# Turning the first half's norms by DMA instead of on TensorE, with the second norm's transfers behind head 4's

## The chip, the cores and the metric

One core of a Trainium2 chip. The metric is the device time of one execution in microseconds; the kernel before took 1820.86 us (median of 3 runs, 1820.22 to 1822.54). The engines of the core work side by side, each through its own queue of instructions in order: TensorE (matmuls, with its weight loads shown apart), VectorE, ScalarE, GpSimd, and SyncE, which here only issues DMA transfers. They meet at semaphores.

## The reference

`x` and a context are 16 batches of 256 rows of 256 numbers. Four residual layers follow each other; the change lies in the first one:

```
x = x + L0_xattn(ctx, layernorm(x), ...)      # first half
x = x + L0_ffn(layernorm(x), ...)             # second half, from here on
x = x + L1_xattn(layernorm(x), ctx, ctx, ...)
x = x + L1_ffn(layernorm(x), ...)             # 8 experts, routed

def L0_xattn(x, latents, ...):
    xn = layernorm(x) * gamma_media + beta_media
    ln = layernorm(latents) * gamma_lat + beta_lat
    q  = ln @ Wq + bq
    k, v = split(concat([xn, ln]) @ Wkv + bkv)      # 512 rows of keys and values
    out = softmax(q k^T / sqrt(128)) v              # 8 heads of width 128
    return out @ Wo + bo
```

Here the "media" input is the context (norm 0, `k` = 0 in the code) and the latents are x, normalised twice (norms 1 and 2; the second has `k` = 1 where only two inputs are counted). Gamma and beta belong to columns of the normalised rows.

## The kernel before

**Precision.** Each matmul operand is held as two fp32r halves, a high one (ScalarE rounds) and a low one (VectorE subtracts the high from the full value). A product of two such operands is three matmuls (L741 to L743).

**The first half** (`latent_attention`) has a turn for each batch b of 16. Within it eight heads follow each other. In head h's step TensorE computes the scores of head h+1 (`sim`), then the step's products into a ring of four PSUM banks, in the order of `slot`: K of head h+2, Q in even steps, O of head h-1, V. From head 6 on, K, Q and V are already those of batch b+1. ScalarE takes exps and high halves, VectorE maxima, low halves and inverses of row sums, GpSimd the normalisation of the probabilities. The probabilities go from rows to columns by DMA: GpSimd writes a high f16 part (L411), VectorE the low one (L665), SyncE issues a transposing transfer for each (`cross`, L323), ScalarE casts both back to fp32r (`casts`, L512). `cross(b, h)` waits for the part to be made and for the cast that frees its buffer.

**The norms of batch b+1** are made in turn b: statistics on VectorE in steps 0 to 2, the norm's application on GpSimd (`norm_apply`, L400) in the same steps. In step 4, after the first product, TensorE transposes both norms (`transposes`, L752: eight 128x128 transposes into the banks `ps_c` and `ps_x`). ScalarE applies gamma and beta out of these banks into `aff` (L459, two activations for each norm, after the second and third product of step 4). In step 5 VectorE splits `aff` into `kvh` and `kvl` (`kv_halves`, L591 and L593): for norm 0 ahead of the step's products, for norm 1 after the first. TensorE waits for both (`kv_ready`) before the first product of step 6, K of head 0 of the next batch.

**Order and extras.** Nothing reorders these queues; they are written out. In turns 1 to 8 (the `spare` loop) one expert's weights of the second half are loaded, split by ScalarE (steps 0 to 2) and VectorE (L1891, steps 1 to 3) and stored. Turn 14 prepares the second half (`ahead`), and turn 15 has no next batch and runs work of the second half beside its own (`beside`). There the probabilities are transposed on TensorE. GpSimd fills the second half's weights in `early`, `ahead` and `beside`: rank-one updates, then an accumulating DMA (`weights_added`, L1258).

**The end of the first half.** TensorE projects the last batch out in four groups, with the second half's products at the marks `("W", 0)` and `("W", 1)`: the transposes of that half's norm C, and the products that need them.

The second half already turns its own norm A by DMA in the same manner: `ln_parts`, `ln_turned`, L1734, L1208, L1430.

## Time and profile before

| | |
|---|---|
| median of 3 runs | 1820.86 us |
| the profiled execution | 1820.83 us, span 1818.9 us |
| TensorE, matmuls | 1785.6 us busy, 98% |
| VectorE | 1467.5 us, 81% |
| ScalarE | 1329.6 us, 73% |
| GpSimd | 548.0 us, 30% |
| granted TensorE clock | full in every slice |

The span is cut into engines' busy times; TensorE's matmuls overlap, so its busy share is not its distance to its peak. The first half ends at about 984 us. In timelines a row gives the start, the duration, the engine and line, the operation and its output and input, and in brackets the idle time of the engine before it and what ended it. Two starts that follow each other give the pitch, which is shorter than the duration because instructions overlap.

### The profile page before, as it was taken

Reading aid. Unit: us, or ns where it says so; the run is one execution under the profiler, and the core shown is the slowest. Engines: PE = TensorE matmul, PEld = TensorE weight load, DVE = VectorE, ACT = ScalarE, POOL = GpSimd, SP = SyncE. Lnnn points to the kernel's source line nnn. Section 1 sums busy time; section 2 is a strip of 40 time slices with the busy share of each in tenths; the row PEclk is TensorE's granted clock in tenths of the full one; section 3 lists DMA queues with packets and bytes.
Section 4 is the critical chain, followed back from the end, with each engine's and each line's share of the span. In section 5 each row is a group of like instructions: output and inputs, shape, how many; then the busy total and the mean of one; then the engine's idle time right before and its main releaser. Section 6 shows DMA issues by size and latency. Waiting matters only on the chain.

```text
span 1818.9 us, 40134 instructions
## 1 busy us (share of the span) xinstructions
PE 1785.6 (98%) x12818; PEld 1658.1 (91%) x12818; DVE 1467.5 (81%) x3544; ACT 1329.6 (73%) x2554; POOL 548.0 (30%) x714
## 2 busy tenths in 40 slices
PE   7999999999999999999999999999999999999999
PEld 5888888888888888888888999999999999999998
DVE  7888888888888878888667888888888888888876
ACT  5778777877887777777777767777767777776653
POOL 3454434543345433454542111101111110111100
PEclk9999999999999999999999999999999999999999
DMA  5565555545555444444529534333443434344300
GB/s 151 109 134 124 124 135 133 148 103 145 133 133 99 87 93 86 97 96 91 117 68 311 147 66 95 72 88 72 83 94 66 95 69 90 72 83 89 72 7 13
DMA packets 370652, 185.92 MB, mean 102 GB/s; under 512 B 307744, under 2 KB 355744, under 8 KB 370592
## 3 DMA queue, kind: packets, MB, share of 16 engines
q1 hardware_dynamic: 361888, 150.55, 34.9%
q0 software_dynamic: 8704, 34.61, 10.5%
q8 instruction: 33, 0.54, 0.1%
q14 instruction: 27, 0.22, 0.0%
HBM read 97.29 MB, written 21.23 MB: 65 GB/s over the span
## 4 chain that ended last, share of the span: by engine, by line
PE 81%; DVE 8%; ACT 4%; issue 4%; DMA 2%; POOL 1%; SPq 0%; DVEq 0%; ACTq 0%; POOLq 0%
PE ring L741 9%; PE ring L743 9%; PE ring L742 9%; PE ring L2087 8%; PE ring L2089 8%; PE ring L2088 8%; PE sim L2089 3%; PE sim L2087 3%; PE sim L2088 3%; PE sim L741 3%; PE sim L742 2%; PE sim L743 2%; PE ps_x L741 2%; PE ps_x L742 2%; PE ps_x L743 2%
## 5 line engine op out<-in xcount | busy, mean ns | idle before, releaser
L411 POOL TENSOR_SCALAR a_parts<-a_pr,a_rinv 128x512 f16<-128x512 f32 x240 | 177.8, 752 | 468.3 <-DVE a_rinv L656 420.0
L2087 PE MATMUL ring<-b_xch,b_wel 128*128 128x256 f32 x1024 | 288.6, 282 | 0.5 <-DVE b_act_e L1701 0.5
L2089 PE MATMUL ring<-b_xcl,b_weh 128*128 128x256 f32 x1024 | 286.4, 280 | 0.0
L2088 PE MATMUL ring<-b_xch,b_weh 128*128 128x256 f32 x1024 | 286.2, 279 | 0.0
L2088 PEld LDWEIGHTS ring<-b_xch,b_weh 128*128 128x128 f32 x1024 | 193.4, 189 | 0.0
L2087 PEld LDWEIGHTS ring<-b_xch,b_wel 128*128 128x128 f32 x1024 | 192.2, 188 | 0.7 <-DVE b_act_e L1701 0.7
L2089 PEld LDWEIGHTS ring<-b_xcl,b_weh 128*128 128x128 f32 x1024 | 192.0, 188 | 0.0
L504 ACT ACTIVATE a_pr<-sim,a_nmax 128x512 f32<-128x512 f32 x256 | 173.7, 688 | 19.4 <-DVE a_nmax L645 18.8
L1407 ACT ACTIVATE b_heh<-b_act_e 128x512 fp32r<-128x512 f32 x128 | 80.9, 632 | 136.0 <-DVE b_act_e L1701 114.6
L665 DVE SCALAR_TENSOR_TENSOR a_parts<-a_pr,a_rinv,a_parts 128x512 f16<-128x512 f32 x240 | 178.8, 786 | 0.0
L645 DVE TENSOR_REDUCE a_nmax<-sim 128x1 f32<-128x512 f32 x256 | 165.0, 682 | 9.8 <-PE sim L743 9.8
L741 PE MATMUL ring<-a_pth,a_vh 128*128 128x256 f32 x512 | 146.4, 286 | 1.9 <-ACT a_ptl L512 0.5
L512 ACT ACTIVATE a_ptl<-a_turned 128x1024 fp32r<-128x1024 f16 x120 | 127.0, 1058 | 26.1 <-DMA a_turned<-a_parts 26.0
L492 ACT ACTIVATE a_vh<-ring 128x512 fp32r<-128x512 f32 x128 | 77.0, 601 | 90.9 <-PE ring L743 90.9
L742 PE MATMUL ring<-a_ptl,a_vh 128*128 128x256 f32 x512 | 143.0, 279 | 0.0
L743 PE MATMUL ring<-a_pth,a_vl 128*128 128x256 f32 x512 | 142.9, 279 | 0.0
L1227 POOL TENSOR_SCALAR b_rows<-b_mv 128x2 f32<-128x2 f32 x48 | 12.5, 260 | 430.7 <-DVE b_mv L1641 430.5
L632 DVE TENSOR_TENSOR a_vl<-ring,a_vh 128x512 fp32r<-128x512 f32 x128 | 88.2, 689 | 59.5 <-ACT a_vh L492 59.4
L623 DVE SCALAR_TENSOR_TENSOR a_ktl<-ring,a_bkv_s,a_kth 128x512 fp32r<-128x512 f32 x128 | 96.0, 750 | 48.0 <-ACT a_kth L484 46.0
L1701 DVE TENSOR_TENSOR b_act_e<-b_act_e,ring 128x512 f32<-128x512 f32 x128 | 87.6, 684 | 51.7 <-PE ring L2089 39.1
L512 ACT ACTIVATE a_pth<-a_turned 128x1024 fp32r<-128x1024 f16 x120 | 127.3, 1061 | 2.3 <-DMA a_turned<-a_parts 2.2
L1403 ACT ACTIVATE b_act_e<-ring 128x512 f32<-128x512 f32 x128 | 76.1, 595 | 60.6 <-PE ring L2089 60.3
(369 smaller groups left out, 6473.6 us busy)
## 6 DMA issues: line engine op xcount, KB each, us to landing
b_w2l_raw<-in_W2T POOLq DMA_DIRECT2D x16, 1088.0 KB, 8.8
b_even_b<-rows_between SPq DMA_DIRECT2D x16, 1024.0 KB, 5.5
b_w1l_raw<-in_W1T POOLq DMA_DIRECT2D x16, 1024.0 KB, 8.4
b_w1l_raw<-in_We SPq DMA_DIRECT2D x8, 768.0 KB, 4.6
expert_halves<-b_w1h SPq DMA_DIRECT2D x8, 768.0 KB, 3.5
expert_halves<-b_w1l SPq DMA_DIRECT2D x8, 768.0 KB, 4.9
b_weh<-expert_halves SPq DMA_DIRECT2D x8, 768.0 KB, 8.7
b_wel<-expert_halves SPq DMA_DIRECT2D x8, 768.0 KB, 10.2
```

The source lines that it names most:

```text
L411: nc.gpsimd.tensor_scalar(parts[:, 0, t, :], pr[:, h % 2, t, :], rinv[:, h % 2, t:t + 1], 1.0, ALU.mult, ALU.mult).then_inc(prob_ready, 1)
L504: nc.scalar.activation(pr[:, h % 2, t, :], sim[t][:], ACT.Exp, bias=nmax[:, h % 2, t:t + 1], accum_out=rsum[:, h % 2, t:t + 1]).then_inc(e ...
L512: nc.scalar.activation(dst[:].rearrange("p k (t q) -> p t k q", t=ST), turned[:, part], ACT.Copy, scale=1.0 / PART_SCALE).then_inc(cast, 1)
L623: nc.vector.scalar_tensor_tensor(ktl[:, h % 2], bank[:], bkv_s[:, 0, h:h + 1], f32(kth[:, h % 2]), ALU.add, ALU.subtract).then_inc(ring_lo, 1)
L645: nc.vector.tensor_reduce(nmax[:, h % 2, t:t + 1], sim[t][:], AX.X, ALU.max, negate=True)\
L665: nc.vector.scalar_tensor_tensor(parts[:, 1, t, :], pr[:, h % 2, t, :], rinv[:, h % 2, t:t + 1], parts[:, 0, t, :], ALU.mult, ALU.subtract ...
L741: nc.tensor.matmul(out, lh, rh, start=(begins and n == 0), stop=False)
L742: nc.tensor.matmul(out, lh, rl, start=False, stop=False)
L743: last = nc.tensor.matmul(out, ll, rh, start=False, stop=(ends and n == len(parts) - 1))
L2087: nc.tensor.matmul(out, ll, rh, start=(n == 0), stop=False)
L2088: nc.tensor.matmul(out, lh, rh, start=False, stop=False)
L2089: last = nc.tensor.matmul(out, lh, rl, start=False, stop=(n == len(parts) - 1))
```

## The change

- `ln_crossing` reserves 8704 bytes in the region `low` for f16 parts of both norms (`a_ln_parts`), their turned form (`a_ln_turned`), and gamma divided by 2^11 (`gms`, `gls`).
- For batches 1 to 15 TensorE no longer transposes the norms; only batch 0's stay there.
- GpSimd writes the high part of norm 0 in step 0 and that of norm 1 in step 3 (`ln_high`). VectorE writes the low parts after step 2's last product and after step 4's second (`ln_low`).
- SyncE issues two transfers for each norm, those of norm 0 behind head 2's probabilities and those of norm 1 behind head 4's (`ln_cross`).
- ScalarE applies gamma and beta to the turned high part after the last product of steps 3 and 5 (`affine_high`).
- VectorE adds the turned low part times gamma, then splits (`joined_halves`), for norm 0 ahead of step 5's products, for norm 1 after the second product.
- The wait for `x1_ready` moves to the projection in step 5. On GpSimd eight memsets move to the begin of the last turn, and `weights_added(0, "1")` from step 7 to step 6 of turn 14. At the end of the first half the mark `("W", 0)` comes right after the first group of projections.

```diff
+        def ln_cross(b, k):
+            take(kv_ready, b * 2 - 1 + k)
+            for part in range(2):
+                take(ln_part, (b - 1) * 4 + 2 * k + part + 1)
+                sp.dma_start_transpose(ln_turned[:, k, part].rearrange("p t c q -> p (t c) q"),
+                                       ln_parts[:, k, part].rearrange("p t d -> p (t d)")).then_inc(lnT_ready, 16)
...
                 if nxt and h + 1 < H:
                     cross(b, h + 1)
+                if nxt and h in (1, 3):
+                    ln_cross(b + 1, h // 2)
...
+        def ln_high(b, k):
+            take(ln_ready, b * 3 + 2 * k + 1)
+            if k == 1:
+                take(ln_part, (b - 1) * 4 + 2)
+            nc.gpsimd.tensor_scalar(ln_parts[:, k, 0], (c_ln, x_ln2)[k][:], LN_SCALE, 1.0, ALU.mult, ALU.mult)\
+                .then_inc(ln_part, 1)
...
                 if nxt and h < 3:
                     rstd_of(b + 1, h)
                     norm_apply(b + 1, h)
+                    if h == 0:
+                        ln_high(b + 1, 0)
+                if nxt and h == 3:
+                    ln_high(b + 1, 1)
...
+        def affine_high(b, k):
+            g, bb = ((gms, bm), (gls, bl))[k]
+            act.wait_ge(lnT_ready, (b - 1) * 64 + 2 + 32 * k + 32)
+            for c in range(DC):
+                last = nc.scalar.activation(aff[:, k, c, :].rearrange("p (t q) -> p t q", t=ST), ln_turned[:, k, 0, :, c, :],
+                                            ACT.Identity, bias=bb[:, c:c + 1], scale=g[:, c:c + 1])
             last.then_inc(aff_ready, 1)
...
-                    if j == 1 and h == H - 4 and nxt:
-                        affine(b + 1, 0)
-                    if j == 2 and h == H - 4 and nxt:
-                        affine(b + 1, 1)
+                    if j == n - 1 and h == 3 and nxt:
+                        affine_high(b + 1, 0)
+                    if j == n - 1 and h == H - 3 and nxt:
+                        affine_high(b + 1, 1)
...
+        def ln_low(b, k):
+            dve.wait_ge(ln_part, (b - 1) * 4 + 2 * k + 1)
+            nc.vector.scalar_tensor_tensor(ln_parts[:, k, 1], (c_ln, x_ln2)[k][:], LN_SCALE, ln_parts[:, k, 0],
+                                           ALU.mult, ALU.subtract).then_inc(ln_part, 1)
+
+        def joined_halves(b, k):
+            done = (b - 1) * 4 + 2 + 2 * k
+            dve.wait_ge(aff_ready, b * 2 + k + 1)
+            for c in range(DC):
+                last = nc.vector.scalar_tensor_tensor(
+                    aff[:, k, c, :].rearrange("p (t q) -> p t q", t=ST), ln_turned[:, k, 1, :, c, :], (gms, gls)[k][:, c:c + 1],
+                    aff[:, k, c, :].rearrange("p (t q) -> p t q", t=ST), ALU.mult, ALU.add)
+            last.then_inc(kv_hi, 1)
+            dve.wait_ge(kv_hi, done + 1)
+            nc.vector.tensor_copy(kvh[:, :, k * S:(k + 1) * S], aff[:, k]).then_inc(kv_hi, 1)
+            dve.wait_ge(kv_hi, done + 2)
             nc.vector.tensor_tensor(kvl[:, :, k * S:(k + 1) * S], aff[:, k], f32(kvh[:, :, k * S:(k + 1) * S]),
                                     ALU.subtract).then_inc(kv_ready, 1)
...
-                    kv_halves(b + 1, 0)
+                    joined_halves(b + 1, 0)
...
-                    if j == 0 and h == H - 3 and nxt:
-                        kv_halves(b + 1, 1)
+                    if j == 1 and h == H - 3 and nxt:
+                        joined_halves(b + 1, 1)
...
+                    if j == n - 1 and h == 2 and nxt:
+                        ln_low(b + 1, 0)
+                    if j == 1 and h == 4 and nxt:
+                        ln_low(b + 1, 1)
...
-                    if j == 0 and h == H - 4 and nxt:
-                        if prev:
-                            pe.wait_ge(x1_ready, b)
-                        transposes(b + 1)
...
+                other.beside(H, ("W", 0))
                 project_out(b, order, i + 1, 1, range(H - 1))
                 project_out(b, order, i + 1, 0, range(H - 1, H))
-                other.beside(H, ("W", 0))
                 project_out(b, order, i + 1, 1, range(H - 1, H))
```

## Rows read from the trace of the kernel before

**Rows 1.** The page: busy times, and the chain that ended last by engine.

```profile
PE 1785.6 (98%) x12818; PEld 1658.1 (91%) x12818; DVE 1467.5 (81%) x3544; ACT 1329.6 (73%) x2554; POOL 548.0 (30%) x714
PE 81%; DVE 8%; ACT 4%; issue 4%; DMA 2%; POOL 1%; SPq 0%; DVEq 0%; ACTq 0%; POOLq 0%
```

**Rows 2.** Windows: stretch, length, busy (count) PE PEld DVE ACT POOL, clock, DMA.

```profile
734.60:791.60 57.00, 56.97 (x346) 49.98 (x346) 46.35 (x99) 44.00 (x85) 25.12 (x30) 1.00 0.44 92
448.80:506.50 57.70, 57.38 (x346) 50.08 (x345) 48.31 (x101) 45.74 (x88) 25.27 (x30) 1.00 0.55 132
```

**Rows 3.** Timeline of TensorE in a plain turn, at heads 4, 5 and 6.

```profile
748.14 0.60 PE L752 MATMUL ps_c<-ident,a_c_ln 128*128 128x128 f32 x4
...
748.93 0.36 PE L741 MATMUL ring<-a_kvh,a_wqh 128*128 128x256 f32 x1
749.13 0.28 PE L742 MATMUL ring<-a_kvl,a_wqh 128*128 128x256 f32 x1
...
755.75 0.39 PE L743 MATMUL ring<-a_kvh,a_wkl 128*128 128x512 f32 x1
756.16 0.38 PE L741 MATMUL ring<-a_pth,a_vh 128*128 128x256 f32 x1
...
761.88 0.39 PE L741 MATMUL ring<-a_kvh,a_wkh 128*128 128x512 f32 x1
```

**Rows 4.** VectorE there, heads 3 to 6, and the low parts' line from 740 to 750.

```profile
744.40 0.75 DVE L623 SCALAR_TENSOR_TENSOR a_ktl<-ring,a_bkv_s,a_kth 128x512 fp32r<-128x512 f32 x1 [0.59 <-ACT a_kth L484]
...
750.09 0.75 DVE L623 SCALAR_TENSOR_TENSOR a_ktl<-ring,a_bkv_s,a_kth 128x512 fp32r<-128x512 f32 x1 [0.21 <-ACT a_kth L484]
...
751.50 0.88 DVE L627 SCALAR_TENSOR_TENSOR a_qtl<-ring,a_bq_s,a_qth 128x256 fp32r<-128x256 f32 x2 [0.39 <-ACT a_qth L488]
752.90 0.69 DVE L632 TENSOR_TENSOR a_vl<-ring,a_vh 128x512 fp32r<-128x512 f32 x1 [0.53 <-ACT a_vh L492]
754.17 0.48 DVE L639 SCALAR_TENSOR_TENSOR a_otl<-ring,a_bkv_s,a_oth 128x256 fp32r<-128x256 f32 x1 [0.58 <-ACT a_oth L497]
754.57 1.28 DVE L645 TENSOR_REDUCE a_nmax<-sim 128x1 f32<-128x512 f32 x2
...
757.09 0.42 DVE L591 CAST a_kvh<-a_aff 128x512 fp32r<-128x512 f32 x1
757.55 0.69 DVE L593 TENSOR_TENSOR a_kvl<-a_aff,a_kvh 128x512 fp32r<-128x512 f32 x1
...
759.57 0.69 DVE L593 TENSOR_TENSOR a_kvl<-a_aff,a_kvh 128x512 fp32r<-128x512 f32 x1
...
L665 DVE SCALAR_TENSOR_TENSOR a_parts<-a_pr,a_rinv,a_parts x4: 740/752/1194, 742.4 to 749.1; 128x512 f16<-128x512 f32 x4
```

**Rows 5.** ScalarE in the same turn: head 3's low cast, norm 1's affine.

```profile
747.07 1.06 ACT L512 ACTIVATE a_ptl<-a_turned 128x1024 fp32r<-128x1024 f16 x1
...
752.74 1.04 ACT L459 ACTIVATE a_aff<-ps_x,a_bl,a_gl 128x256 f32<-128x256 f32 x2
```

**Rows 6.** The second half's instructions of this kind (min/median/max in ns).

```profile
L1734 DVE SCALAR_TENSOR_TENSOR b_ln_parts<-b_ln,b_ln_parts x14: 681/684/686, 1023.9 to 1715.3; 128x512 f16<-128x512 f32 x14
L1430 ACT ACTIVATE b_xth<-b_ln_turned x14: 632/632/635, 1028.1 to 1720.6; 128x512 fp32r<-128x512 f16 x14
```

**Rows 7.** The probabilities' transfers: SyncE's issue (ns), and time to landing.

```profile
L323 SPq DMA_TRANSPOSE a_turned<-a_parts x240: 1231/1232/2204, 31.8 to 888.5; - x120
...
DMA to landing us min/median/max: 3.1/3.1/4.9
```

**Rows 8.** An expert turn: ScalarE and VectorE at head 4, TensorE at head 6.

```profile
289.24 1.07 ACT L512 ACTIVATE a_ptl<-a_turned 128x1024 fp32r<-128x1024 f16 x1 [1.03 <-DMA a_turned<-a_parts]
...
292.25 0.75 DVE L623 SCALAR_TENSOR_TENSOR a_ktl<-ring,a_bkv_s,a_kth 128x512 fp32r<-128x512 f32 x1 [0.54 <-ACT a_kth L484]
...
303.41 0.39 PE L741 MATMUL ring<-a_kvh,a_wkh 128*128 128x512 f32 x1
```

**Rows 9.** TensorE at the end of the first half, waiting for norm C.

```profile
983.30 0.39 PE L2178 MATMUL sim<-b_xch,b_wr 128*128 128x256 f32 x1 [1.12 <-DVE b_xcl L1730]
```

More of the change, by code:

```diff
@@ L78, in crossing, with ln_crossing @@
         return Region(low.nc, (low.top + 127) // 128 * 128 + 2 * 8 * KB + 64, 8 * KB)
+    def ln_crossing(self):
+        low = self.of["low"]
+        return Region(low.nc, (low.top + 127) // 128 * 128 + 2 * 8 * KB + 64 + 8704, 8704)
 @dataclass
@@ L397, in norm_apply @@
             if k != 1:
-                take(lnT_ready, b * 2 - 1 + k // 2)
+                take(lnT_ready, (b - 1) * 64 + 2)
             for t in range(ST):
@@ L460, in affine @@
                                             bias=bb[:, c:c + 1], scale=g[:, c:c + 1])
+            last.then_inc(aff_ready, 1)
+        def affine_high(b, k):
[4 more added lines that the diff above has]
+                                            ACT.Identity, bias=bb[:, c:c + 1], scale=g[:, c:c + 1])
             last.then_inc(aff_ready, 1)
@@ L822, in project_out @@
                 last.then_inc(wo_full, 1)
-        pe.wait_ge(consts, 1)
+        pe.wait_ge(pool_step, 3)
         transposes(0)
@@ L884, in fill_count @@
         return last.at(at + last.names[at:].index(name)) + 1
-    names = ("consts", "kv_ready", "x1_ready", "x1_out", "ring_full", "ring_lo", "sim_full", "exp_done", "wo_full", "took",
+    names = ("kv_ready", "x1_ready", "x1_out", "ring_full", "ring_lo", "sim_full", "exp_done", "wo_full", "took",
              "part_hi", "part_lo", "turned")
-    sems = dict(zip(names, (consts, kv_ready, x1_ready, x1_out, ring_full, ring_lo, sim_full, exp_done, wo_full, took,
+    sems = dict(zip(names, (kv_ready, x1_ready, x1_out, ring_full, ring_lo, sim_full, exp_done, wo_full, took,
                             prob_ready, part_lo, turned_lo)))
@@ L1270, in early @@
                 for e in range(E):
-                    nc.gpsimd.memset(index[:, e:e + 1], float(e))
-                for c in range(HC):
-                    last = nc.gpsimd.memset(f32(w2_raw[:, c * W2ROW + D:(c + 1) * W2ROW]), 0.0)
+                    last = nc.gpsimd.memset(index[:, e:e + 1], float(e))
                 last.then_inc(consts, 1)
@@ L1287, in ahead @@
                 update(0, "1", 3)
+                weights_added(0, "1")
             if h == 7:
-                weights_added(0, "1")
                 rows_rstd(1)
@@ L1293, in beside @@
             if (h, done) == (0, "begin"):
+                pool.wait_ge(first.sems["kv_ready"], 2 * B)
+                for c in range(HC):
+                    nc.gpsimd.memset(f32(w2_raw[:, c * W2ROW + D:(c + 1) * W2ROW]), 0.0)
                 update(0, "2", 0)
```

19 lines of the change are left out of this document (14 added, 5 removed).

## The prediction

> **What bounds the kernel now.** I read the page first: TensorE is busy 98% of the span and carries 81% of the chain that ended last, with VectorE next at 8% [rows 1]. Then the busy times of whole turns of the first half [rows 2]. A turn is one batch of heads: 57.0 us for batches whose turn has nothing extra, 57.7 us for the eight turns that also split expert weights. TensorE has 56.97 us of work in the 57.0, so there the turn is as long as TensorE's queue. VectorE has 46.35 us and ScalarE 44.00: slack on average, which says nothing of a single head. So I read the timelines of TensorE, VectorE and ScalarE over heads 2 to 6 of one plain turn (batch near 734 to 792 us) and of one expert turn (near 276 to 334 us). What the reader is to see there: where VectorE and ScalarE have no idle gap left (a bracket on a row is the idle time before it), because the change takes work from TensorE and gives it to exactly these two.
>
> **What leaves TensorE.** The eight 128x128 transposes stand between the K and the Q product of head 4: from 748.14 to 748.93 us, 0.79 us [rows 3]. The product behind them starts 0.20 us before its successor instead of the usual 0.12: 0.87 us in all. A second piece: at head 5 the O product starts 0.41 us after the last K product (755.75 to 756.16), where 0.23 is the pitch of such a product [rows 3]; it had waited for ScalarE's cast of the low probabilities, which was late because the two affine pairs (1.04 us, 0.9 to the next start, the second at 752.74 [rows 5]) had pushed it. They move to heads 3 and 5, so these 0.18 us, and 0.10 of a slow first matmul behind them, are free as well. TensorE's own queue gets 1.15 us shorter per turn, 15 turns: 17.3 us. That is the most the edit can bring in the first half.
>
> **What VectorE gets.** Two low halves of the norms (`ln_low`) and, in `joined_halves`, four scalar_tensor_tensors of 128x256, which add the turned low half to the affine before the two instructions that were there already. `ln_low` is the instruction that the second half has: 0.684 us [rows 6], 0.60 to the next start. Back-to-back instructions of VectorE start about 0.09 us before the one ahead ends (0.48 long, 0.40 to the next start: 754.17 to 754.57 [rows 4]); the sums below go by such pitches. No row shows a 128x256 one that reads f16 from SBUF. The nearest is the Q pair, 0.88 us for two [rows 4]; the next instruction waits for its result, which costs 0.04 more (as from 757.09 + 0.42 to 757.55 [rows 4]): 0.92 us a pair. Bounds: not less than the 0.42 us of the cast over the same 512 elements, not more than 1.3, since one 512-element instruction with two inputs reached 1.19 us beside GpSimd [rows 4].
>
> **Head 2 and 3.** `ln_low(0)` sits behind head 2's last product, in front of the maxima of head 4 (741.20). The gap of 0.59 us before K's low half (744.40) takes it up for K [rows 4], but the low probability parts of head 3, between the two, end 0.60 us later, and their transfer lands 3.1 us behind its issue [rows 7]. SyncE also has the norm's second transfer in front: ready at 741.2 + 0.68 = 741.9, 1.23 us of issue each for it and for head 3's high part, so free again at 744.5, just when the low parts are (744.4): no cost, but no slack. ScalarE gets the first affine pair ahead of head 3's two casts: 0.7 us from the f16 source (the second half's 512-element one takes 0.632 [rows 6]). Bounds: 0.63 to the 0.9 of today. Its low cast (747.07, without idle time in front [rows 5]) starts 0.7 us later by either of the two, which overlap. Everything behind it on ScalarE shifts: exps of head 5, then K's high half, whose taker on VectorE goes from 750.09 to 750.79. Bounds of the shift: 0 (if the cast had slack) to 1.3 (both in series).
>
> **Head 4.** From K's low half to the maxima of head 6 VectorE now needs 0.66 (K), 0.29 (inverses), 0.79 (Q), 0.61 (V), 0.40 (O) and the new 0.60: 3.35 us. The three waits there today (0.39 on ScalarE's Q half, 0.53 and 0.58 [rows 4]) came from the affine pairs and from TensorE's transposes and go. Maxima of head 6: 754.14 instead of 754.57 [rows 4].
>
> **Head 5, where it is decided.** TensorE may not start the next batch's K product (761.88 today [rows 3]) before both halves of the keys' input are split. Today this is done at 759.57 + 0.69 = 760.26 [rows 4], 1.6 us early. Now from 754.14: maxima 1.20, parts 1.32, first joined halves 0.92 + 1.07, K's low 0.66, inverses 0.29, O's low 0.40 (the second joined halves stand behind it now), second joined halves 0.92 + 0.46 + 0.69: 7.93 us, so 762.07. With 0.15 for the wake-up and 0.10 for the slower first product TensorE goes on as if from 762.32. Without the wait it would be there at 760.73. So 1.6 us of new idling eat the 1.15 saved: +0.44 us a turn. VectorE's later gaps at heads 6 and 7 let it catch up, so the next turn starts in the same posture.
>
> **Expert turns.** VectorE there has no gap from head 1 to head 4. The low cast of head 3 already waits 1.03 us for its transfer [rows 8] and comes 0.60 later; K's low half 292.25 becomes 292.85; + 3.35 + 7.93 = 304.13; + 0.25 = 304.38 against 303.41 [rows 8]: +0.97 us. Its two stalls before the scores of heads 4 and 5 only move inside this.
>
> **The rest.** GpSimd gets two 128x512 conversions while it idles most of the span (30% busy [rows 1]): nothing; without that cover the probabilities of one head would be late by such a conversion. Issues of four more transfers a turn: nothing, as reckoned above; uncovered, each would be 1.23 us on the path of a cast. Two 128x2 activations at the start: under 0.5 us, beside loads. At the seam `weights_added` moves one step up on GpSimd; its issue and the next head's normalisation only swap places ahead of the row statistics for which VectorE waits, so the end of the three is the same: nothing. The eight small memsets go where GpSimd soon waits for VectorE: nothing. The last change moves the transposes of the final norm in front of 21 projection products (21 x 0.117 = 2.5 us); the 1.12 us that TensorE waits after them today and its restart [rows 9] go: -1.3 us, once.
>
> **Sum.** 8 expert turns x 0.97 = 7.8 (batch 0's turn, loaded with weight splits, counted as plain), 7 others x 0.44 = 3.1, seam -1.3: +9.6 us. The profiled execution took 1820.83 us around its span of 1818.9; the median of the runs is 1820.86, the same. Forecast 1830.4 us.
>
> **A rule weighed.** The longest of four low-part instructions took 1.194 us against a median of 0.752 [rows 4], and such pairs fall where GpSimd works. The Trainium skill, page "GPSIMD Engine Reference", Specifications, says that GpSimd shares its SBUF interfaces with VectorE and that they collide when a VectorE instruction has two SBUF inputs. The row agrees. By the rule the joined pairs, which run beside GpSimd's normalisation of heads 5 and 6, would be slow as well, and the sum would be the third rival's 1842; by the quiet row it stays at 1830.4.
>
> **Rivals.** (1) *The shift at head 3 is absorbed* (transfer and affine fit into slack that the timeline doesn't show): 0.7 and 0.6 less. Plain turns -0.26, expert turns +0.37: 7 x -0.26 + 8 x 0.37 - 1.3 = -0.2 us, 1820.6. For it: the cast follows its neighbour without a gap, so a small change of order could hide it; against it: the same in expert turns is plainly a wait for the transfer. (2) *Faster: the split is ready before TensorE asks.* It decides at the next batch's K product: if the chain of 7.93 us and what precedes it is 1.6 us shorter in plain turns, TensorE keeps the 1.15. The pairs at 0.42 give 1.0 of it, the absorbed shift 0.7: together enough. Then 15 x 1.15 + 1.3 = 18.6 us less; the expert turns, whose chain is 0.5 us longer, keep about 0.5 of it less (4 us): 1806. With only half of that margin, 1814. For it: VectorE's average load; against: no row with so cheap a pair. (3) *Slower still: the added two-input instructions collide with GpSimd*, pairs at 1.3: 0.76 more per turn, 11.4 us, 1842. For: the 1.194 row; against: only a part of them lies beside GpSimd. (4) *Transfers in SyncE's queue bound head 3*: a norm transfer lands or issues late (the second half's take longer under load) and the head's low part behind it by 1 us: +15, 1845.
>
> **Chances.** Forecast 0.52 (own range 1824.5 to 1838), rival 1 0.19, rival 2 with its half 0.19, rivals 3 and 4 together 0.10. No change is within 0.2%, 3.6 us, about what a measurement of this kernel can tell. Faster 0.19, same 0.20, slower 0.61. The range 1811 to 1841 leaves out the full rival 2 (0.09) and the tail of rivals 3 and 4 (0.06).
>
> **What would show it.** Right: the first-half 128x128 transposes fall from 128 to 8; TensorE idles about 1.6 us (less its restart) before the next batch's K product, released by VectorE's last `a_kvl`; the O product of head 5 no longer lags; head 3's low cast starts later; a turn lasts 57.4 plain and 58.6 with experts; the second half keeps its length. Wrong: turns of 56 us, or the wait at another product (scores of head 5 on `a_ktl`, O on the cast), or joined pairs away from 0.92 us.

## The result: 1841.9 us, 1.2% slower

The changed kernel took 1841.88 us (median of 4, 1840.66 to 1845.51), the kernel before 1821.51 beside it: ratio 1.0118, 95% interval [1.0106, 1.0130]. The forecast was 1830.4 us, the range 1811 to 1841. The sign and the place of the new wait were right; the loss was twice the forecast one (+20.4 us against +9.6).

The page after: busy times, and the chain that ended last, as [rows 1].

```profile
PE 1776.8 (97%) x12698; PEld 1645.7 (90%) x12698; DVE 1522.0 (83%) x3634; ACT 1331.0 (72%) x2556; POOL 574.7 (31%) x744
PE 63%; DVE 17%; issue 7%; ACT 5%; DMA 4%; SPq 2%; POOL 1%; DVEq 0%; ACTq 0%; POOLq 0%
```

120 transposes are gone from TensorE, and VectorE's share of the chain has doubled, from 8 to 17%. Where the time went is told by turns, from one write of `x_out` on VectorE to the next (differences to before, where the expert turns are 57.5 to 57.7 and the plain ones 56.9 to 57.1):

| stretch | after minus before, us |
|---|---|
| up to the first write | +3.6 |
| the turn after it (the first with an expert) | +2.0 |
| the 7 other expert turns | +8.2 (1.17 each) |
| 5 plain turns | +8.7 (1.74 each) |
| turn 14 and the last turn | -2.3 |
| all up to the last write | +20.1 |

The span grew by 19.9 (1818.9 to 1838.8), so in this execution the second half kept its length (the section on e7 comes back to that). Windows after of one plain and one expert turn, columns as in [rows 2]:

```profile
752.80:811.60 58.80, 56.55 (x337) 49.20 (x336) 50.20 (x105) 44.28 (x85) 27.21 (x32) 1.00 0.48 98
282.80:341.50 58.70, 56.60 (x337) 49.11 (x336) 51.81 (x108) 45.53 (x88) 26.65 (x32) 1.00 0.59 138
```

VectorE has 3.5 to 3.9 us more in a turn, ScalarE as much as before; VectorE's slack on average is still 7 to 9 us. TensorE's waits from 60 to 900 us (us in total, times, longest), after:

```profile
PE ring L807 <- DVE a_kvl L655: 16.2, 13, 1.7
PE sim L807 <- DVE a_qtl L689: 8.0, 16, 1.9
PE sim L807 <- DVE a_ktl L685: 7.9, 9, 0.9
PE ring L807 <- ACT a_ptl L554: 2.6, 3, 1.5
```

The first row did not exist before: it is the forecast wait for the keys' input. In the same stretch of before the second was 0.8 us, once, and the third 2.4 us in 8. In the plain turn TensorE shows two waits, at the scores of head 6 and at K of the next batch (against 761.88 in [rows 3]; by the write of `x_out` at its head 1 this turn lies 18.86 us later than the one shown of before). At 767.32 Q follows K without the transposes, and at 775.10 O follows K at its usual pitch:

```profile
767.09 0.39 PE L809 MATMUL ring<-a_kvh,a_wkl 128*128 128x512 f32 x1
767.32 0.28 PE L807 MATMUL ring<-a_kvh,a_wqh 128*128 128x256 f32 x1
...
772.23 0.49 PE L807 MATMUL sim<-a_kth,a_qth 128*128 128x512 f32 x1 [0.54 <-DVE a_qtl L689]
...
774.87 0.39 PE L809 MATMUL ring<-a_kvh,a_wkl 128*128 128x512 f32 x1
775.10 0.28 PE L807 MATMUL ring<-a_pth,a_vh 128*128 128x256 f32 x1
...
782.49 0.50 PE L807 MATMUL ring<-a_kvh,a_wkh 128*128 128x512 f32 x1 [1.64 <-DVE a_kvl L655]
```

Both kernels run the same 336 other matmuls in a turn, in the same order. Laid beside each other from the write of `x_out`, the changed one gains and loses at five products (changed minus before, us, with the slower first matmuls behind a wait):

| TensorE's product | the plain turn | an expert turn (from 282.8) |
|---|---|---|
| scores of head 5 | +0.33 | +0.60 |
| Q in step 4, the transposes gone | -0.87 | -0.88 |
| scores of head 6 | +0.80 | +0.55 |
| O in step 5 | -0.28 | -0.29 |
| K of the next batch | +1.92 | +1.21 |
| sum | +1.90 | +1.19 |

VectorE in the plain turn, to be laid beside [rows 4]:

```profile
760.05 0.82 DVE L640 SCALAR_TENSOR_TENSOR a_ln_parts<-a_c_ln,a_ln_parts 128x512 f16<-128x512 f32 x1
...
762.00 1.64 DVE L727 SCALAR_TENSOR_TENSOR a_parts<-a_pr,a_rinv,a_parts 128x512 f16<-128x512 f32 x2
...
770.26 0.75 DVE L685 SCALAR_TENSOR_TENSOR a_ktl<-ring,a_bkv_s,a_kth 128x512 fp32r<-128x512 f32 x1 [1.24 <-ACT a_kth L526]
...
772.01 0.87 DVE L640 SCALAR_TENSOR_TENSOR a_ln_parts<-a_x_ln,a_ln_parts 128x512 f16<-128x512 f32 x1
...
773.79 1.27 DVE L707 TENSOR_REDUCE a_nmax<-sim 128x1 f32<-128x512 f32 x2
...
776.31 0.87 DVE L648 SCALAR_TENSOR_TENSOR a_aff<-a_ln_turned,a_gms,a_aff 128x256 f32<-128x256 f16 x2
777.21 0.43 DVE L653 CAST a_kvh<-a_aff 128x512 fp32r<-128x512 f32 x1
...
779.63 1.23 DVE L648 SCALAR_TENSOR_TENSOR a_aff<-a_ln_turned,a_gls,a_aff 128x256 f32<-128x256 f16 x2
780.90 0.81 DVE L653 CAST a_kvh<-a_aff 128x512 fp32r<-128x512 f32 x1
781.74 0.69 DVE L655 TENSOR_TENSOR a_kvl<-a_aff,a_kvh 128x512 fp32r<-128x512 f32 x1
```

Read the two joined pairs against each other: 0.87 us for the first, 1.23 for the second, and its cast 0.81 instead of 0.43. GpSimd and ScalarE beside them (the affine and low cast as in [rows 5]):

```profile
771.65 1.79 POOL L438 TENSOR_SCALAR a_parts<-a_pr,a_rinv 128x512 f16<-128x512 f32 x2 [1.48 <-DVE a_rinv L718]
779.66 1.76 POOL L438 TENSOR_SCALAR a_parts<-a_pr,a_rinv 128x512 f16<-128x512 f32 x2 [6.22 <-DVE a_rinv L718]
```

```profile
764.93 1.08 ACT L499 ACTIVATE a_aff<-a_ln_turned,a_bm,a_gms 128x256 f32<-128x256 f16 x2
...
767.25 1.06 ACT L554 ACTIVATE a_ptl<-a_turned 128x1024 fp32r<-128x1024 f16 x1 [0.29 <-DMA a_turned<-a_parts]
```

GpSimd's normalisations of heads 5 and 6 start with the low half of norm 1 and with the second pair; where they stand alone such a pair of GpSimd's takes 1.36 us, here 1.79 and 1.76. Both sides pay. In expert turns the second pair and its cast are quick, and GpSimd's normalisation of head 6 starts only behind them:

```profile
310.24 0.87 DVE L648 SCALAR_TENSOR_TENSOR a_aff<-a_ln_turned,a_gls,a_aff 128x256 f32<-128x256 f16 x2
311.15 0.43 DVE L653 CAST a_kvh<-a_aff 128x512 fp32r<-128x512 f32 x1
```

```profile
312.58 1.36 POOL L438 TENSOR_SCALAR a_parts<-a_pr,a_rinv 128x512 f16<-128x512 f32 x2 [8.54 <-DMA a_turned<-a_parts]
```

The norms' own transfers (issue in ns, time to landing), as [rows 7]:

```profile
L340 SPq DMA_TRANSPOSE a_ln_turned<-a_ln_parts x60: 1188/1189/2262, 48.2 to 891.7; - x60
...
DMA to landing us min/median/max: 2.4/2.4/4.2
```

### The profile page after: what moved, and what is told of

Same layout as the page of the kernel before. It is cut to its first block, busy times and chain, and to the rows that moved or that the text cites. A ratio compares the mean times of both kernels' runs of the same rounds, so it can differ in the third digit from the quotient of the medians.

```text
span 1838.8 us, 40340 instructions
## 1 busy us (share of the span) xinstructions
PE 1776.8 (97%) x12698; PEld 1645.7 (90%) x12698; DVE 1522.0 (83%) x3634; ACT 1331.0 (72%) x2556; POOL 574.7 (31%) x744
## 3 DMA queue, kind: packets, MB, share of 16 engines
q0 software_dynamic: 8704, 34.61, 10.5%
## 4 chain that ended last, share of the span: by engine, by line
PE 63%; DVE 17%; issue 7%; ACT 5%; DMA 4%; SPq 2%; POOL 1%; DVEq 0%; ACTq 0%; POOLq 0%
PE ring L2151 8%; PE ring L2153 8%; PE ring L2152 8%; PE ring L807 6%; PE ring L809 6%; PE ring L808 6%; DVE a_parts L727 3%; PE sim L2153 3%; PE sim L2151 3%; PE sim L2152 3%; DVE a_nmax L707 2%; DMA a_turned<-a_parts 2%; DVE a_aff L648 1%; PE ps_x L2151 1%; PE ps_x L2153 1%
## 5 line engine op out<-in xcount | busy, mean ns | idle before, releaser
L727 DVE SCALAR_TENSOR_TENSOR a_parts<-a_pr,a_rinv,a_parts 128x512 f16<-128x512 f32 x240 | 186.6, 817 | 3.2 <-DMA a_turned<-a_parts 1.9
L685 DVE SCALAR_TENSOR_TENSOR a_ktl<-ring,a_bkv_s,a_kth 128x512 fp32r<-128x512 f32 x128 | 95.8, 749 | 58.9 <-ACT a_kth L526 58.8
L807 PE MATMUL sim<-a_kth,a_qth 128*128 128x512 f32 x256 | 105.5, 412 | 20.1 <-DVE a_ktl L685 10.3
```

Of the source, the lines that this page charges most:

```text
L685: nc.vector.scalar_tensor_tensor(ktl[:, h % 2], bank[:], bkv_s[:, 0, h:h + 1], f32(kth[:, h % 2]), ALU.add, ALU.subtract).then_inc(ring_lo, 1)
L727: nc.vector.scalar_tensor_tensor(parts[:, 1, t, :], pr[:, h % 2, t, :], rinv[:, h % 2, t:t + 1], parts[:, 0, t, :], ALU.mult, ALU.subtract ...
L807: nc.tensor.matmul(out, lh, rh, start=(begins and n == 0), stop=False)
```

## The experiments

Differences are to the kernel before, measured beside each run (1819.4 to 1821.0 us); the changed kernel itself stands at +20.4. "Expert" and "plain" are the mean lengths of the 7 and 5 such turns of the table above in the profiled run (before 57.6 and 57.0, changed 58.8 and 58.8). e4, e7 and e12 are edits of the kernel before, the others of the changed one.

| run | edit | us | minus before | ratio, 95% interval | expert / plain |
|---|---|---|---|---|---|
| e4 | before, fewer transposes | 1812.5 | -7.1 | 0.9960 [0.9946, 0.9974] | 57.4 / 56.3 |
| e1 | no low halves | 1828.9 | +9.2 | 1.0049 [1.0032, 1.0066] | 57.7 / 57.9 |
| e2 | no joining | 1830.7 | +11.0 | 1.0063 [1.0047, 1.0080] | 58.2 / 57.6 |
| e3 | GpSimd waits, head 6 | 1836.2 | +16.5 | 1.0089 [1.0073, 1.0106] | 58.6 / 57.8 |
| e5 | low half 0 in step 1 | 1839.3 | +19.4 | 1.0102 [1.0086, 1.0119] | 58.5 / 58.6 |
| e9 | e5, bias in step 7 | 1841.9 | +20.8 | 1.0110 [1.0093, 1.0127] | 58.6 / 58.8 |
| e10 | e9 and e3 | 1836.4 | +15.4 | 1.0086 [1.0070, 1.0103] | 58.5 / 57.8 |
| e13 | e9, affine in a gap | 1837.7 | +18.2 | 1.0096 [1.0079, 1.0113] | 58.5 / 58.0 |
| e14 | e13, low half 1 in a gap | 1833.1 | +13.7 | 1.0063 [1.0047, 1.0080] | 58.3 / 57.6 |
| e15 | e14 and e3 | 1826.1 | +6.6 | 1.0033 [1.0022, 1.0045] | 58.3 / 56.8 |
| e17 | e15, low half 1 on GpSimd | 1827.1 | +6.8 | 1.0038 [1.0024, 1.0052] | 58.1 / 56.8 |
| e18 | e17, low half 0 too | 1826.7 | +6.4 | 1.0031 [1.0020, 1.0041] | 57.8 / 57.2 |
| e16 | e15, splits in step 6 | 1846.3 | +26.8 | 1.0142 [1.0125, 1.0159] | 60.6 / 56.9 |
| e8 | gamma, beta in rows | 1851.1 | +31.2 | 1.0161 [1.0141, 1.0181] | 59.7 / 58.4 |
| e11 | e8 spread | 1969.4 | +148.4 | 1.0808 [1.0790, 1.0826] | 68.8 / 64.4 |
| e6 | e5, affine, joining early | 1915.4 | +95.6 | 1.0516 [1.0497, 1.0534] | 63.8 / 63.5 |
| e7 | before, mark moved | 1820.3 | +0.4 | 1.0004 [0.9994, 1.0014] | 57.6 / 56.9 |
| e12 | before, bias in step 7 | 1820.8 | -0.2 | 0.9999 [0.9989, 1.0009] | 57.7 / 57.0 |

### What TensorE's saving is worth (e4)

```diff
-                        last = nc.tensor.transpose(ps[...], ln[:, t, c * P:(c + 1) * P], ident[:])
+                        if isinstance(b, int) and b == 0 or c == DC - 1 and t == ST - 1:
+                            last = nc.tensor.transpose(ps[...], ln[:, t, c * P:(c + 1) * P], ident[:])
```

> The kernel before with 2 of the 8 transposes of each batch from 1 on, one of each norm: six blocks of each batch's input stay those of batch 0, which leaves that part of the computation out. It measures what TensorE's saved time is worth where nothing is put in its place. Theory A (TensorE's queue sets the turn): six transposes of about 0.1 us each are 0.59 us a turn, 15 turns: 8.9 us less than 1821.5: 1812.6. Rival E (TensorE's saved time is lost anyway, because VectorE and ScalarE set the turn): 1821.

Six of eight transposes of each later batch are gone, and with them most of the turned norms: that part of the computation is left out. -7.1 us is 0.5 a turn, but it isn't spread evenly. Plain turns gain 0.75 us, so there the gain side of the change is real. Expert turns gain only 0.22: TensorE now waits 0.40 us in each for ScalarE's low cast, ahead of the O product of step 5. There a part of the saving is lost even with nothing put in its place.

### Taking one added cost away at a time (e1, e2, e3)

```diff
# e1: low halves over 4 elements only (but for the first batch)
+            n = D if isinstance(b, int) and b == 1 else 2
+            ... (c_ln, x_ln2)[k][:, :, 0:n], LN_SCALE, ln_parts[:, k, 0, :, 0:n], ...
# e2: joining over 2 elements only
+                    aff[:, k, c, 0:2], ln_turned[:, k, 1, 0, c, 0:2], (gms, gls)[k][:, c:c + 1], ...
# e3: GpSimd, ahead of the normalisation of head 6
+                if nxt and h == H - 3:
+                    take(kv_ready, b * 2 + 4)
```

> The changed kernel with VectorE's two low halves of the norms (ln_low) cut from 512 to 4 elements for all batches but the first turned one; transfers, joins and everything else stay. The rows joined are then partly old ones: that part of the computation is left out. Theory A (the loss comes from VectorE's chain: low half of norm 0 ahead of head 3's low probabilities, then the low half of norm 1 in head 4, each 0.75 to 0.79 us to the next start): 2 x 0.7 us less for each of 15 turns, 21 us less than the changed kernel's 1841.9: 1820 us, turns of 57.3 us. Rival B (the four more transfers in SyncE's queue set the end of head 3, the low half of norm 0 costs nothing): only norm 1's counts, 0.75 x 15 = 11 us less: 1831. Rival C (TensorE's stalls have another cause): 1842.

> The changed kernel with the four scalar_tensor_tensors per batch that add the turned low part (in joined_halves) cut from 256 to 2 elements: the low part of the norms is left out of the result. Theory A: the first pair costs 0.90 and the second, beside GpSimd, 1.27 us, and the cast behind it 0.38 more than it need: up to 2.2 us a turn come off the way to the next batch's K product, where TensorE idles 1.8 to 1.9 us in a plain turn and 1.2 in an expert turn; what is left is the stalls at the scores of heads 5 and 6 and TensorE's own queue of 55.9 us. 1841.9 less 7 x 1.8 and 8 x 1.2, 22 us: 1820 us. Rival B (the stall at that product is only moved, the scores' stalls grow): 1830 or more.

> The changed kernel, with one wait more: GpSimd starts the normalisation of head 6's probabilities only when VectorE has split the second norm (kv_ready), so that the two don't run side by side. The computation is whole. Theory A (collision of GpSimd with VectorE's two-input instructions costs 0.36 us in the second joined pair and 0.38 in the cast behind it): 0.74 x 15 = 11 us less than 1841.9: 1831 us, turns of 58.0 us, joined pair back at 0.87 us. Rival C (these instructions are slow by themselves at that place): 1842 and the same durations. Rival D (the later normalisation delays head 6's probabilities by 1.5 us and gives it all back): 1842 or more with the pair at 0.87.

Against the changed kernel's +20.4 the low halves are worth 11 us, the joining 9, the collision in step 5 alone 4: each about a third to a half of what theory A gave it. In every one of the three TensorE still waits for the last low half. No single term carries the loss; each lies on the same path. e1 and e2 leave a part of the computation out; in e3 nothing is, only GpSimd's one normalisation is later. Its plain turns fall by 0.9 us, of which the pair and the cast, back at 0.87 and 0.43, give 0.35 and 0.38; its expert turns, which had no such collision, fall by 0.1.

### A chain over two engines (e5, e9, e13, e14, e15)

```diff
# e5: VectorE's low half of norm 0
-                    if j == n - 1 and h == 2 and nxt:
+                    if j == n - 1 and h == 1 and nxt:
                         ln_low(b + 1, 0)
```

> The changed kernel, but norm 0's low half is made behind the last product of step 1 instead of step 2, so that its two transfers leave SyncE's queue before those of head 3's probabilities. Theory A (in plain turns half of the unforeseen loss comes from head 3: the low half in front of the maxima and the norm's second transfer in front of head 3's push its low cast by 1.3 us, and VectorE then idles 1.24 us at head 4 for K's high half): plain turns fall by 1.0 to 1.3 us, expert turns, where VectorE has no gap at head 1 either, by 0.3 to 0.5; about 1829. Rival B (only VectorE's load over heads 4 and 5 counts, the shift at head 3 is taken up anyway): less than 0.3 per turn, 1837 to 1841.

Only 0.15 to 0.25 a turn in the profiled run, and 1.0 us in the medians, which their spread doesn't separate. VectorE's wait of 1.24 us at head 4 was indeed gone, but the time was spent one instruction earlier. VectorE and GpSimd in e5:

```profile
765.16 2.62 DVE L727 SCALAR_TENSOR_TENSOR a_parts<-a_pr,a_rinv,a_parts 128x512 f16<-128x512 f32 x2
768.14 0.75 DVE L685 SCALAR_TENSOR_TENSOR a_ktl<-ring,a_bkv_s,a_kth 128x512 fp32r<-128x512 f32 x1 [0.36 <-ACT a_kth L526]
```

```profile
764.92 0.62 POOL L428 TENSOR_SCALAR a_ln_parts<-a_x_ln 128x512 f16<-128x512 f32 x1
765.62 1.61 POOL L448 TENSOR_TENSOR a_x_res<-a_x_res,a_bo_b 128x512 f32<-128x512 f32 x1
```

I took the 2.62 us (1.41 where GpSimd rests) for the cause and moved the bias addition away:

```diff
# e9
-                if h == 3:
+                if h == (7 if nxt else 3):
                     bias_residual(b, prev)
```

> The kernel with norm 0's low half in step 1 (1839.3) plus one move on GpSimd: the addition of the output bias to the residual (128x512, two inputs, 1.6 us) from step 3 to step 7. Theory A (VectorE's added instructions and its old two-input ones are slow because GpSimd works beside them; in that kernel the low parts of head 4 took 2.62 us for two beside this addition, and K's product of the next batch waits for what stands behind them): 0.8 to 1.2 us less per plain turn, 0.3 to 1.0 per expert turn; 1826 to 1830. Rival B (the pair is long because it waits for something else, the addition only lies beside it): 1838 to 1840.

The pair is quick again, and nothing is won: theory A fell. VectorE in e9, then ScalarE:

```profile
765.73 1.49 DVE L727 SCALAR_TENSOR_TENSOR a_parts<-a_pr,a_rinv,a_parts 128x512 f16<-128x512 f32 x2
768.71 0.75 DVE L685 SCALAR_TENSOR_TENSOR a_ktl<-ring,a_bkv_s,a_kth 128x512 fp32r<-128x512 f32 x1 [1.49 <-ACT a_kth L526]
```

```profile
763.29 0.60 ACT L534 ACTIVATE a_vh<-ring 128x512 fp32r<-128x512 f32 x1 [0.86 <-PE ring L809]
763.79 1.08 ACT L499 ACTIVATE a_aff<-a_ln_turned,a_bm,a_gms 128x256 f32<-128x256 f16 x2
764.77 1.04 ACT L554 ACTIVATE a_pth<-a_turned 128x1024 fp32r<-128x1024 f16 x1
765.72 1.04 ACT L554 ACTIVATE a_ptl<-a_turned 128x1024 fp32r<-128x1024 f16 x1
...
768.00 0.68 ACT L526 ACTIVATE a_kth<-ring,a_bkv_s 128x512 fp32r<-128x512 f32 x1
```

Here the path is in view. ScalarE waits 0.86 us for TensorE's V product of head 3; from there it has no gap through V's high half, the affine of norm 0 (0.98), two casts, the exps of head 5 and K's high half at 768.00. VectorE takes over at 768.71 and has no gap until the last low half. What is put between costs its full length; what is moved inside costs nothing. The 0.98 stands just behind the gap that could have hidden it:

```diff
# e13: ScalarE's affine of norm 0 ahead of V in step 3
-                    if j == n - 1 and h == 3 and nxt:
+                    if j == 1 and h == 3 and nxt:
                         affine_high(b + 1, 0)
# e14: VectorE's low half of norm 1 ahead of step 4's products
-                    if j == 1 and h == 4 and nxt:
-                        ln_low(b + 1, 1)
+                if h == 4 and nxt:
+                    ln_low(b + 1, 1)
```

e10 is e9 with e3's wait, e15 is e14 with it.

> As the run before (bias addition in step 7), and GpSimd's normalisation of head 6 waits until the joined halves are done, so that it no longer lies beside the second joined pair and its cast. Theory A (the same collisions, 1.0 us more per plain turn, little in expert turns, as the run with this wait alone showed): 7 us less than the run before, about 1820. Rival B (once the low parts of head 4 are quick, head 5 is no longer decided by VectorE's chain): within 2 us of the run before.

> The kernel with norm 0's low half in step 1 and the bias addition in step 7 (1841.9, turns of 58.55 with experts and 58.75 without) and one more move: ScalarE's affine of norm 0 before V's high half of head 3, where it idled 0.86 us for TensorE, instead of after it. Theory A (one serial chain over ScalarE and VectorE from V of head 3 to the next batch's K product decides; the affine stands in it with 0.98 us): plain turns 0.8 to 0.9 us less, expert turns 0.4 to 0.8; 1830. Rival B (the two engines are simply short of time in heads 3 to 5, order doesn't matter): 1840 to 1842.

> As the run before, and VectorE's low half of norm 1 ahead of step 4's products, where VectorE waits for ScalarE's K, instead of behind the second. Theory A: of 0.79 us the 0.5 that is still idle there is won, 0.5 per turn; 1824. Rival B: no change against the run before, since K's low half is pushed by as much.

> As the run before, and GpSimd's normalisation of head 6 waits for the joined halves (no collision in head 5; that wait alone took 5 us off in two earlier pairs of runs). Theory A: plain turns 56.4 to 56.9, expert turns 57.6 to 57.9; 1816 to 1820, at or just under the kernel before. Rival B: head 7 is late by the delayed probabilities once head 5 is no longer so, 1822 or more.

e10 gives 5.4 us over e9: the collision counts about as in e3 (3.9), not more. In e9, e13, e14 and e15 plain turns fell step by step, 58.8, 58.0, 57.6, 56.8, each within about 0.1 us of what theory A gave (0.8 to 0.9, 0.5, then the collision), and ended under the 57.0 of before. Expert turns did not follow: 58.6, 58.5, 58.3, 58.3. So the medians missed theory A each time: 1837.7 for 1830, 1833.1 for 1824, 1826.1 for 1816 to 1820. TensorE and VectorE in the plain turn of e15: the low half in the gap takes 0.68 instead of 0.87, and the pair and cast of norm 1 their undisturbed 0.87 and 0.43.

```profile
769.29 0.50 PE L809 MATMUL ring<-a_kvh,a_wkh 128*128 128x512 f32 x1 [0.56 <-DVE a_kvl L657]
```

```profile
757.45 0.68 DVE L642 SCALAR_TENSOR_TENSOR a_ln_parts<-a_x_ln,a_ln_parts 128x512 f16<-128x512 f32 x1
...
767.17 0.87 DVE L650 SCALAR_TENSOR_TENSOR a_aff<-a_ln_turned,a_gls,a_aff 128x256 f32<-128x256 f16 x2
768.08 0.43 DVE L655 CAST a_kvh<-a_aff 128x512 fp32r<-128x512 f32 x1
```

### Why expert turns don't follow (e16, e17, e18)

```diff
# e16: VectorE's second and third split in step 6, the stores in SyncE's step 7
-            if h in (1, 2, 3):
+            for n in {1: (0,), 6: (1, 2)}.get(h, ()):
# e17: the scale goes into the reciprocal deviation, GpSimd makes norm 1's low half in step 3
+            nc.gpsimd.tensor_tensor(ln_parts[:, k, 1], (c_ln, x_ln2)[k][:], ln_parts[:, k, 0],
+                                    ALU.subtract).then_inc(ln_part, 1)
# e18: and norm 0's in step 1
```

> As the run before, and in expert turns the second and third split of expert weights on VectorE in step 6 instead of steps 2 and 3 (their stores to DRAM in step 7 instead of 4). Theory A (expert turns lack the gaps of heads 2 and 3): expert turns become like plain ones, 0.6 to 1.0 less each, 1810 to 1813. Rival B (heads 6 and 7 have no room for 1.2 us either): no change.

e16 tells nothing of its question: the later stores stand in SyncE's way. Its issue of the next load comes at 273.7, 4.9 us behind the last store's, with the probabilities' transfers behind it, and TensorE waits up to 1.7 us, before scores, early in the turn that follows.

> The kernel with all moves (1826.1; turns of 58.35 with experts, 56.8 without), and the low half of norm 1 made by GpSimd behind the high half in step 3 instead of by VectorE in step 4 (the scale of 2^11 goes into the reciprocal deviation). Theory A (VectorE's serial work up to the last low half of the keys' input decides in both kinds of turn): expert turns 0.5 to 0.7 less, plain turns 0.4 to 0.6 until TensorE's own queue of 56.1 to 56.4 bounds; 1817 to 1820. Rival B (what VectorE is spared, the two-input instruction on GpSimd takes back by collision with the low parts of head 4): 1824 or more.

> As the run before, and norm 0's low half by GpSimd as well, behind its norm work in step 1. Theory A (expert turns also lose at the scores of heads 3 to 5 because VectorE has no gap in heads 1 to 4): expert turns another 0.3 to 0.6 less, plain ones unchanged; 1813 to 1817, faster than the kernel before. Rival B (GpSimd has 1.3 to 1.8 us of room in step 1, and the probabilities of head 3 come late): 1820 or more.

With both low halves off VectorE expert turns come to 57.8 us, near the 57.6 of before; with norm 1's alone off to 58.1. e1, which leaves the low halves out, has 57.7. So the two low halves, in heads where VectorE has no gap, are what held them. But GpSimd's two-input instruction takes part of it back: in e17 the low parts of head 4 lie beside it and last 2.40 us instead of 1.70 in e15, and plain turns gain nothing (in e18 they lose 0.4). VectorE in e15, then VectorE and GpSimd in e17:

```profile
755.83 1.70 DVE L729 SCALAR_TENSOR_TENSOR a_parts<-a_pr,a_rinv,a_parts 128x512 f16<-128x512 f32 x2
```

```profile
754.86 2.40 DVE L737 SCALAR_TENSOR_TENSOR a_parts<-a_pr,a_rinv,a_parts 128x512 f16<-128x512 f32 x2
```

```profile
755.23 1.49 POOL L435 TENSOR_TENSOR a_ln_parts<-a_x_ln,a_ln_parts 128x512 f16<-128x512 f32 x1
```

The profiled run of e18 is 7.1 us longer than that of before. 3.5 of them lie up to the second write of `x_out`, 1.2 in the expert turns (0.8 of that in one disturbed turn), 0.7 in the plain ones, -0.8 in turn 14 and the last, and 2.4 behind the last write of `x_out`, where the next section finds them again. In e15 it is 4.5 up to the last write and 3.1 behind it. Why the first turns, loaded with weight splits, cost more was not tried.

### Three ways that went wrong (e6, e8, e11)

```diff
# e6: e5, affine of norm 0 at the end of step 2, its joining at the end of step 3
# e8: GpSimd, on c_ln and x_ln2, g and b as rows of all 128 partitions
+                nc.gpsimd.tensor_tensor(dst[:], dst[:], g_row, ALU.mult)
+                nc.gpsimd.tensor_tensor(dst[:], dst[:], b_row, ALU.add)
# after the turn ScalarE casts the high half into kvh, VectorE the low one into kvl
# e11: these four in steps 1 to 3, all halves and transfers in steps 3 and 4
```

> As the run before (low half in step 1), and the affine of norm 0 behind the last product of step 2 and its two added two-input instructions behind the last product of step 3; only the split stays in step 5. Theory A (head 5 is decided by the chain on VectorE from the maxima to the last low half; 0.87 us less stand in it, but they are done at head 3 or 4, where VectorE has next to no gap left): 0.2 to 0.6 per plain turn better than the run before, nothing in expert turns; about 1827. Rival B (steps 3 and 4 have a gap that takes it whole): 0.87 x 15 = 13 us better than the run before, 1816.

> All norms of batches 1 to 15 by DMA, but gamma and beta are applied to the rows on GpSimd before the split into halves, so that after the turn ScalarE only casts the high half into the keys' input and VectorE the low half (behind step 5's second product); no affine and no joining. Low half of norm 0 in step 1. Theory A (the chain on VectorE in heads 4 and 5 is what costs; TensorE's saving of 1.15 us a turn comes through once it is gone): turns of 56.0 to 56.4 plain, 57.0 expert, 1804 with a range of 1801 to 1810. Rival B (turning by DMA costs by its transfers and by GpSimd's added work beside VectorE): 1815 or more.

> Gamma and beta applied to the rows on GpSimd, as in the run that took 1851.1 us, but GpSimd's four additions and multiplications (1.3 us each) are spread over steps 1 to 3, the high halves written in steps 3 and 4, the low halves at the ends of steps 3 and 4, the transfers in steps 3 and 4, the bias addition in step 7. After the turn only two casts on ScalarE and two on VectorE, in step 5. Theory A (that run was slow because GpSimd's norm work in steps 0 and 2 pushed the probabilities of heads 2 and 4): turns of 56.3 to 57.2; 1806 to 1815. Rival B (each two-input instruction on GpSimd costs VectorE more than it spares, wherever it stands): 1825 or more.

ScalarE in e6, then TensorE in e11 (us in total, times, longest):

```profile
ACT a_aff L499 <- DMA a_ln_turned<-a_ln_parts: 44.0, 13, 3.6
```

```profile
PE ring L809 <- DVE a_kvl L657: 43.2, 13, 4.9
```

In e6 SyncE's queue has head 2's probabilities in front of the norm, so ScalarE stood still for the transfer with casts and exps behind it. In e8 the four instructions take 1.3 us each beside 2.9 for a norm, GpSimd has only about 2 us of room in steps 0 to 2, and the probabilities are late: ScalarE waits 72 us for their transfers and TensorE 31 us for Q's low half. In e11 the halves and with them the keys' input are late. Rival B was nearer in e8 and e11; that it was GpSimd's own queue rather than collisions is read from these waits and not shown by a run. A part of e11 and e6 is TensorE's clock: in their first halves the granted clock averaged 0.91 to 0.97 and 0.95 to 0.99 of full by stretches of 60 us and more, where it was 1.00 before. How much of the loss that makes was not told apart.

### The other edits of the change (e7, e12)

```diff
# e7, on the kernel before
+                other.beside(H, ("W", 0))
                 project_out(b, order, i + 1, 1, range(H - 1))
                 project_out(b, order, i + 1, 0, range(H - 1, H))
-                other.beside(H, ("W", 0))
```

> The kernel before with nothing but the mark of the second half's norm at the end of the first half moved behind the first group of projections. Theory A (the wait of 1.12 us and its restart go, nothing else): 1818.5, 1.3 less than the kernel before; the stall of 2.6 us in turn 14 stays. Rival B (the edit only moves the wait): no difference, 1819.7.

> The kernel before with the bias addition on GpSimd in step 7 instead of step 3. Theory A (in the kernel before the same collision is there, but VectorE has the slack to take it in plain turns; expert turns have a stall of 0.3 to 0.5 us before the scores of head 5): 1 to 4 us less, 1817. Rival B (no slack is touched): 1819.8.

TensorE in e7, where [rows 9] had 1.12 us, and at the next meeting with VectorE; then this meeting before and in the changed kernel:

```profile
980.23 0.28 PE L2178 MATMUL sim<-b_xch,b_wr 128*128 128x256 f32 x1
...
995.86 0.55 PE L2087 MATMUL sim<-b_w2h,b_hl 128*128 128x256 f32 x1 [2.11 <-DVE b_hl L1725]
```

```profile
997.03 0.36 PE L2087 MATMUL sim<-b_w2h,b_hl 128*128 128x256 f32 x1 [0.20 <-DVE b_hl L1725]
```

```profile
1017.20 0.35 PE L2151 MATMUL sim<-b_w2h,b_hl 128*128 128x256 f32 x1 [0.64 <-DVE b_hl L1789]
```

The wait is gone and 2.11 us stand at the next meeting, where there were 0.20. With the mark alone moved, turn 14 and the last are 2.1 us shorter and the stretch behind the last write of `x_out` 2.1 us longer (837.8 for 835.8): it brings nothing. So the -2.3 of the changed kernel in these turns is not a gain of its own either. That its second half still kept its length (835.5) hangs on the 0.64: in every other profiled kernel with the mark moved this wait is 1.6 to 2.3 us and the stretch 836.4 to 838.9. Its profiled execution is the fastest of the four (1840.66 for a median of 1841.88); why it waited less is open. e12 shows that the kernel before takes the collision at head 3 without loss.

## Why the prediction was wrong

**Bound and place: right.** TensorE is the bound only while the split of the keys' input is in time; the new wait is where it was put, at K of the next batch, released by the last `a_kvl`.

**What leaves TensorE, 1.15 us a turn: right.** Product by product the changed kernel gains 0.87 at Q and 0.28 at O, in the plain turn, and 0.88 and 0.29 in the expert turn. The loss lies wholly in what is waited for.

**The failed step: VectorE's chain in heads 3 to 5 of a plain turn**, +0.44 forecast, +1.74 measured, 1.3 us missed. On TensorE 1.6 us of new idling were forecast, all at K; 1.92 came there and 1.13 more at the scores of heads 5 and 6. Laid over the forecast with the 18.86 us between the two turns, the maxima of head 6 were due at 773.00 and came at 773.79, 0.79 late; the chain from there to the last low half was 7.93 us and took 8.64. Together 1.5 us, less 0.1 because TensorE started 0.06 us behind the last low half and not 0.15:
- the chain of head 5, +0.71: the second joined pair 1.23 instead of 0.88, its cast 0.81 instead of 0.42. The first was 0.87, as forecast. I had one price for both, though the third rival named the collision. e3 undoes exactly this and brings 0.9 us a plain turn;
- heads 3 and 4, +0.79: norm 0's low half 0.14 and norm 1's 0.19 longer, the low parts of head 3 at 1.64 for two where 1.41 is usual, ScalarE's affine pair 0.98 to the next start instead of 0.7, and head 3's low cast 1.32 us later instead of 0.7. At head 3 the low cast still waited 0.29 us for its transfer, so "no cost, but no slack" for SyncE's queue was no reckoning; but e5, which clears it, won 0.25 us a turn at most, since ScalarE's affine was the next to bind. e13 shows the affine's part: 0.7 us a plain turn.

**A wait not seen.** The scores of head 6 need Q's low half of step 4, which VectorE makes after K's: 0.54 us in this turn, 8.0 in all from 60 to 900 us. I reckoned only with K and the keys' input.

**Expert turns: +0.97 forecast, +1.17 measured.** Near, and for a reason: there GpSimd's normalisation of head 6 starts behind the joined halves, so the undisturbed price for the pairs holds. Before, the trace has one stall in such a turn, 0.3 us at the scores of head 5, not the two of the prediction; it grew to 0.9, and one of 0.2 to 0.3 came up at head 6.

**The first batch's turn counted as plain: wrong.** Up to the second write of `x_out`, in the first turn and the first with an expert, 5.6 us were lost, where 0.44 + 0.97 stood.

**The seam, -1.3 us: wrong as argued.** The 1.12 us went, and came back at the next meeting with VectorE (e7).

**The rivals.** The third gave 1842 with pairs at 1.3 us; 1841.9 came, by luck. It charged 0.76 in every turn; measured, one pair of two and its cast are slow, in plain turns alone, and e3 puts 4 of the 20 us on that. The Trainium skill, page "GPSIMD Engine Reference", Specifications, says that VectorE collides with GpSimd in a mode that uses both ports as well as with two SBUF inputs. The trace agrees for two inputs (a half of the second pair at 0.83 us for 0.48). The cast has one input and went from 0.43 to 0.81 us beside GpSimd; that it ran in such a mode no run here shows. I had weighed only instructions with two inputs and given the rival 0.10 with the fourth; the 1.194 us row was evidence enough for more. Rival 1 (shift absorbed) is out by the cast at 767.25. Rival 2 (the split ready before TensorE asks) came in no run: even in e15 TensorE waits 0.4 to 0.6 us at K in a plain turn, which falls 0.2 us under the one of before. Rival 4 (SyncE's queue binds at head 3, by 1 us) has at most the 0.25 us a turn of e5.

## What to carry to other kernels

Work taken from the bound engine is worth its length only if what replaces it stays off the path that feeds that engine: follow this path from the bound engine's last result through every engine back to it, and count each added instruction on it at the price it has beside its neighbours, GpSimd's above all. Before adding an instruction, look for the row where its engine waits and put it right there; the same affine cost 0.7 us a plain turn more behind the gap than in front of it. A stall removed is a gain only when the next candidate is known to be later: here an early transfer, a quick pair and a vanished wait each moved the idle time by one instruction.

## What the runs showed of the hardware

- VectorE beside GpSimd: the two-input low half of a norm, 128x512, went from 0.68 to 0.82 and 0.87 us, a pair of 128x256 from 0.87 to 1.23, a one-input cast of 128x512 from 0.43 to 0.81, a pair of low parts from 1.41 to 2.40 (e17) and 2.62 (e5) beside a two-input GpSimd instruction and to 1.6 to 1.8 beside one-input ones (e15).
- GpSimd pays too: its normalisation pair took 1.36 us alone and 1.76 to 1.79 beside VectorE.
- A norm's transfer holds half the bytes of the probabilities' and lands in 2.4 us instead of 3.1, but its issue occupies SyncE for 1.19 us instead of 1.23: between these two sizes the queue is paid by the transfer, not by the byte.
- ScalarE's 128x256 activation from f16 in SBUF is no cheaper than from PSUM in f32: 1.08 us for two against 1.04.
- TensorE's first matmul behind a wait is slower: 128x512 at 0.49 to 0.50 us instead of 0.39, and the matmul after it starts 0.10 to 0.11 us later than usual.
